# Low halves of the probabilities kept dense: products with values on 64 rows each, crossed over two banks

## The reference

```python
q = rope(layernorm(x) @ wq)      # 32 heads of 128
k = rope(ctx @ wk)               # 8 heads, each shared by 4 query heads
v = ctx @ wv                     # 8 heads
attn = softmax(q @ k.T / sqrt(128) + mask)
x = x + tanh(g_xattn) * ((attn @ v) @ wo)
h = layernorm(x)
# one of 8 experts for each position, chosen by the largest logit, of rank 16:
x = x + tanh(g_ffn) * (top_logit * (h @ A[e].T) @ Bw[e].T)
```

## Time and profile before

| | |
|---|---|
| median of 3 runs | 1091.52 us (1091.41 to 1092.5) |
| span of the profiled execution, first to last instruction | 1089.0 us |
| PE busy | 1082.4 us (99%) |
| PE weight loads busy | 919.3 us (84%) |
| DVE busy | 874.1 us (80%) |
| ACT busy | 636.8 us (58%) |
| POOL busy | 591.9 us (54%) |
| share of PE in the chain that ended last | 97% |
| granted TensorE clock | 9 tenths or more in all 40 slices; mean 1.000 |

### The profile page before, as it was taken

The page is one execution under the profiler, slowest core; times in us unless marked ns, Lnnn a source line. Parts: engine busy times, 40 slices in busy tenths (PEclk is TensorE's granted clock), DMA queues, the critical chain, the costliest instruction groups (busy, mean ns, idle before and its releaser), DMA issues.

```text
span 1089.0 us, 17107 instructions
## 1 busy us (share of the span) xinstructions
PE 1082.4 (99%) x5640; PEld 919.3 (84%) x5640; DVE 874.1 (80%) x1423; ACT 636.8 (58%) x1112; POOL 591.9 (54%) x518
## 2 busy tenths in 40 slices
PE   9999999999999999999999999999999999999998
PEld 7888888888888888888888888888888888888886
DVE  7876657888888888888887898777777777777887
ACT  7563476586666666666655545555555555555553
POOL 5552379888877777777754433333333333333423
PEclk9999999999999999999999999999999999999999
DMA  7858964496646464646489546553535353543112
GB/s 258 273 210 336 391 220 183 155 379 201 214 155 213 155 213 156 212 156 212 141 300 380 185 136 205 177 187 111 187 110 187 112 184 114 179 116 118 40 39 78
DMA packets 106087, 206.27 MB, mean 189 GB/s; under 512 B 8849, under 2 KB 58641, under 8 KB 100113
## 3 DMA queue, kind: packets, MB, share of 16 engines
q1 hardware_dynamic: 105424, 204.40, 55.2%
q10 hardware_dynamic: 576, 0.79, 0.2%
HBM read 122.31 MB, written 82.84 MB: 188 GB/s over the span
## 4 chain that ended last, share of the span: by engine, by line
PE 97%; DVE 2%; DMA 0%; issue 0%; ACT 0%; DVEq 0%; SPq 0%
PE attn L945 32%; PE proj L877 28%; PE score L894 10%; PE attn L839 8%; PE score L839 4%; PE turned L839 4%; PE attn L930 3%; PE attn L932 3%; PE turned L905 3%; PE proj L811 1%; PE small L983 1%; PE small L1008 1%; PE score L983 0%; DMA near_raw<-in_ctx 0%; DVE o_s L1270 0%; DVE stats L1140 0%
## 5 line engine op out<-in xcount | busy, mean ns | idle before, releaser
L945 PE MATMUL attn<-wo_s,o_s 128*128 128x512 f32 x1524 | 374.7, 395 | 0.2 <-DVE o_s L1270 0.2
L877 PE MATMUL proj<-xB,wq_s 128*128 128x512 f32 x1344 | 332.6, 391 | 0.0
L945 PEld LDWEIGHTS attn<-wo_s,o_s 128*128 128x128 f32 x1524 | 280.9, 188 | 57.0 <-DVE o_s L1270 0.4
L877 PEld LDWEIGHTS proj<-xB,wq_s 128*128 128x128 f32 x1344 | 252.0, 188 | 51.3 <-issue 0.2
L1863 POOL TENSOR_TENSOR rot<-rot,tab 128x512 f32<-128x512 f32 x110 | 162.3, 1475 | 145.2 <-ACT rot L1584 145.0
L1633 ACT ACTIVATE o_s<-attn 128x512 fp32r<-128x512 f32 x127 | 69.3, 595 | 112.2 <-PE attn L932 112.1
L894 PEld LDWEIGHTS score<-k_r,q_r 128*128 128x128 f32 x1024 | 123.9, 191 | 5.5 <-DVE q_r L1180 0.4
L1175 DVE TENSOR_TENSOR q_r<-q_r,tab 128x512 f32<-128x512 f32 x127 | 120.9, 952 | 1.5 <-ACT x_third L1584 1.4
L894 PE MATMUL score<-k_r,q_r 128*128 128x64 f32 x1024 | 121.3, 271 | 0.0
L1605 ACT ACTIVATE copies<-proj 128x512 f32<-128x512 f32 x96 | 57.5, 599 | 78.0 <-PE proj L877 77.8
L1282 DVE SCALAR_TENSOR_TENSOR acc<-attn,gates_t,acc 128x512 f32<-128x512 f32 x127 | 94.8, 747 | 4.1 <-PE attn L945 1.2
(11 more groups left out here) (269 smaller groups left out, 1681.5 us busy)
## 6 DMA issues: line engine op xcount, KB each, us to landing
wq_kept<-wq_s SPq DMA_DIRECT2D x16, 1792.0 KB, 6.3
wq_s<-wq_kept SPq DMA_DIRECT2D x16, 1792.0 KB, 8.2
v_kept<-vst SPq DMA_DIRECT2D x64, 256.0 KB, 4.3
v_s<-v_kept SPq DMA_DIRECT2D x128, 128.0 KB, 5.0
wo_kept<-wo_s SPq DMA_DIRECT2D x32, 512.0 KB, 5.7
wo_s<-wo_kept SPq DMA_DIRECT2D x32, 512.0 KB, 5.2
k_kept<-kst SPq DMA_DIRECT2D x32, 256.0 KB, 2.2
wq_raw<-in_wq SPq DMA_DIRECT2D x16, 512.0 KB, 7.8
```

Of the source, the lines that this page charges most:

```text
L877: last = e.matmul(dst[:, :], wq_s[:, b % 2, A, s, kt, :], xB[:, B, mv, kt, :], start=(first and kt == 0 and m == 0), stop=(kt == 1 and m = ...
L945: last = e.matmul(out_bank(k, bp)[:, :], o_s[:, s, bp, h, :], wo_s[n % WO_SLOTS][:, m, :], start=(h == 0 and i == 0), stop=(h == GROUP - 1 ...
```

## The change

`p_low` loses its padding: for each pair of sequences it is 256 columns, in which both twins' low halves stand under each other, as they do in `turned`. POOL's memset of the zeros goes. The pass of 512 columns over 128 rows becomes two passes of 256 columns over 64 rows each, twin 0 with rows 0 to 63 of `p_low` and `v_both`, twin 1 with rows 64 to 127. Both twins of a pair write into one bank, and two passes on different rows of the array are not let into one bank at a time. So the passes are crossed: in turn 0 pair 0 does twin 0 (bank `attn0`) and pair 1 twin 1 (bank `attn1`); then PE waits until both have ended (new semaphore `lows_begun`); in turn 1 pair 0 does twin 1 and pair 1 twin 0. `times_values` is split into `times_high` (the passes of 256 columns over 128 rows, unchanged) and `times_low`. `attn_high` now waits for the last passes of both pairs. In DVE's program the two instructions of `prob_low`, which stood apart in most steps, stand together.

```diff
-        p_low = sb_at(base + 131072, "p_low", [P, PAIRS, 2, GROUP * SEQ], F32R)
+        p_low = sb_at(base + 131072, "p_low", [P, PAIRS, GROUP * SEQ], F32R)
...
-            def times_values(k, pairs=range(PAIRS)):
+            def times_high(k, pairs=range(PAIRS)):
...
-                e.wait_ge(probs_low, 2 * k + 2)
...
                     for twin in range(2):
-                        e.matmul(b[:, cols[twin]], v_s[:, u % 2, twin, tiles[bp], :], p_high[:, twin, cols[bp]],
-                                 start=(twin == 0), stop=False, skip_group_check=True)
-                    e.matmul(b[:, :], v_both[:, u % 2, tiles[bp], :], p_low[:, bp].rearrange("p t n -> p (t n)"),
-                             start=False, stop=True, skip_group_check=True).then_inc(values_used, 1)
+                        e.matmul(out_bank(k, bp)[:, TWIN_COLS[twin]], v_s[:, u % 2, twin, sub * PAIRS + bp, :],
+                                 p_high[:, twin, TWIN_COLS[bp]], start=(twin == 0), stop=False, skip_group_check=True)
+
+            def times_low(k):
+                u, sub = divmod(k, SUBS)
+                e.wait_ge(probs_low, k + 1)
+
+                for turn in range(2):
+                    if turn:
+                        e.wait_ge(lows_begun, PAIRS * (k + 1))
+                    for bp in range(PAIRS):
+                        twin = bp if turn == 0 else 1 - bp
+                        rows = TWIN_ROWS[twin]
+                        e.matmul(out_bank(k, bp)[:, TWIN_COLS[twin]], v_both[rows, u % 2, sub * PAIRS + bp, :], p_low[rows, bp],
+                                 start=False, stop=(turn == 1), skip_group_check=True).then_inc((lows_begun, values_used)[turn], 1)
...
-            times_values(k + 1, [0])
+            times_high(k + 1, [0])
             scores(k + 3)
-            times_values(k + 1, [1])
+            times_high(k + 1, [1])
+            times_low(k + 1)
...
-            def prob_low(k, *twins):
...
+            def prob_low(k):
+                e.wait_ge(probs_high, 3 * k + 2)
...
+                for twin, rows in enumerate(TWIN_ROWS):
+                    last = e.tensor_tensor(p_low[rows, :, :], turned[rows, :].rearrange("p (b n) -> p b n", b=PAIRS),
+                                           p_high[rows, twin, :].bitcast(F32).rearrange("p (b n) -> p b n", b=PAIRS), ALU.subtract)
+                last.then_inc(probs_low, 1)
...
-                together = k % 4 == 3 or (k, 6) in EXTRA
-                if not together:
-                    prob_low(k, 0)
+                if not (k % 4 == 3 or (k, 6) in EXTRA):
+                    prob_low(k)
...
-                prob_low(k, *((0, 1) if together else (1,)))
+                if k % 4 == 3 or (k, 6) in EXTRA:
+                    prob_low(k)
...
             def attn_high(k, bp):
-                e.wait_ge(values_used, PAIRS * k + bp + 1)
+                e.wait_ge(values_used, PAIRS * (k + 1))
...
-                if n == ZEROS_BESIDE:
-
-                    e.wait_ge(rope_added, FOUR.stop)
-                    e.memset(p_low[:, :, :, :].bitcast(F32), 0.0).then_inc(zeros_set, 1)
```

More of the change, by code:

```diff
@@ L43 @@
 SPLIT_PRODUCTS = ((0, 0), (0, 1), (1, 0))
+TWIN_COLS = (slice(0, GROUP * SEQ), slice(GROUP * SEQ, 2 * GROUP * SEQ))
 TWIN_ROWS = (slice(0, SEQ), slice(SEQ, 2 * SEQ))
@@ L195 @@
 SCORES_AFTER = 62
-FOUR_UNTIL, ZEROS_BESIDE = 63, 63
+FOUR_UNTIL = 63
 ROPE_BESIDE = {51: (0, 0), 54: (0, 1), 55: (0, 2), 56: (0, 3), 57: (1, 0), 60: (1, 1), 61: (1, 2)}
@@ L430, in build @@
         mix_scaled, out_ready_g = sem("mix_scaled"), sem("out_ready_g")
-        zeros_set, warm_zeros = sem("zeros_set"), sem("warm_zeros")
+        warm_zeros, lows_begun = sem("warm_zeros"), sem("lows_begun")
         power_set, ln_rstd, times_sin, less_max = sem("power_set"), sem("ln_rstd"), sem("times_sin"), sem("less_max")
@@ L906, in turn_probs @@
                 last.then_inc(probs_turned, 1)
-                drained[turned.name] = probs_low, 2 * k + 2
-            def times_values(k, pairs=range(PAIRS)):
-                u, s = divmod(k, SUBS)
-                tiles = [s * PAIRS + bp for bp in range(PAIRS)]
+                drained[turned.name] = probs_low, k + 1
+            def times_high(k, pairs=range(PAIRS)):
+                u, sub = divmod(k, SUBS)
                 e.wait_ge(v_in[u % 2], 80 * (u // 2 + 1))
-                e.wait_ge(probs_low, 2 * k + 2)
                 e.wait_ge(probs_high, 3 * k + 3)
-                cols = [slice(bp * GROUP * SEQ, (bp + 1) * GROUP * SEQ) for bp in range(PAIRS)]
                 for bp in pairs:
@@ L927, in times_values @@
                         e.wait_ge(x1_added, 2 * k - 1 + bp)
-                    b = out_bank(k, bp)
                     for twin in range(2):
-                        e.matmul(b[:, cols[twin]], v_s[:, u % 2, twin, tiles[bp], :], p_high[:, twin, cols[bp]],
-                                 start=(twin == 0), stop=False, skip_group_check=True)
-                    e.matmul(b[:, :], v_both[:, u % 2, tiles[bp], :], p_low[:, bp].rearrange("p t n -> p (t n)"),
-                             start=False, stop=True, skip_group_check=True).then_inc(values_used, 1)
+                        e.matmul(out_bank(k, bp)[:, TWIN_COLS[twin]], v_s[:, u % 2, twin, sub * PAIRS + bp, :],
+                                 p_high[:, twin, TWIN_COLS[bp]], start=(twin == 0), stop=False, skip_group_check=True)
+            def times_low(k):
+                u, sub = divmod(k, SUBS)
+                e.wait_ge(probs_low, k + 1)
[7 more added lines that the diff above has]
+                                 start=False, stop=(turn == 1), skip_group_check=True).then_inc((lows_begun, values_used)[turn], 1)
+            def times_values(k):
+                times_high(k)
+                times_low(k)
             def project_out(k, bp):
@@ L974, in expert @@
                     elif t >= HALF_TILES + 2:
-                        e.wait_ge(probs_low, 2 * STEPS)
+                        e.wait_ge(probs_low, STEPS)
                         e.wait_ge(x1_added, 2 * (STEPS - 1))
@@ L1252, in sum_rows @@
                 e.reciprocal(row_inv[:, k % 2, :], row_sum[:, k % 2, :]).then_inc(inverted, 1)
-            def prob_low(k, *twins):
[L1255 to L1264, removed]
+            def prob_low(k):
+                e.wait_ge(probs_high, 3 * k + 2)
+                if k:
+                    e.wait_ge(values_used, PAIRS * k)
+                else:
+                    e.wait_ge(rope_added, FOUR.stop)
+                for twin, rows in enumerate(TWIN_ROWS):
+                    last = e.tensor_tensor(p_low[rows, :, :], turned[rows, :].rearrange("p (b n) -> p b n", b=PAIRS),
+                                           p_high[rows, twin, :].bitcast(F32).rearrange("p (b n) -> p b n", b=PAIRS), ALU.subtract)
+                last.then_inc(probs_low, 1)
             def attn_low(k, bp):
@@ L1398, in _ @@
                 q_sum(*q)
-            prob_low(0, 0, 1)
+            prob_low(0)
             finish_key(len(JOBS) - 1)
@@ L1463, in _ @@
             add_out(k - 1, 0)
-            prob_low(k, 0, 1)
+            prob_low(k)
             sum_rows(k + 1)
@@ L1470, in _ @@
             mask_scores(k + 2)
-            prob_low(k + 1, 0, 1)
+            prob_low(k + 1)
             add_out(k, 0)
@@ L1482, in _ @@
             expert_norms_end(tiles_of(k)[1:])
-            prob_low(k + 2, 0, 1)
+            prob_low(k + 2)
             sum_rows(k + 3)
@@ L1492, in _ @@
             expert_norms_begin(tiles_of(k + 1)[:1])
-            prob_low(k + 3, 0, 1)
+            prob_low(k + 3)
             expert_norms_begin(tiles_of(k + 1)[1:])
```

## The result

| | before | changed | ratio, 95% interval |
|---|---|---|---|
| median of runs, us | 1091.47 (1090.84 to 1092.5) | 1127.91 (1125.49 to 1128.5) | 1.0327 [1.0313, 1.0342] |
| span of the profiled execution, us | 1089.0 | 1126.7 | |
| PE busy, us | 1082.4 | 1112.9 | |
| DVE busy, us | 874.1 | 874.9 | |
| ACT busy, us | 636.8 | 636.7 | |

A forecast was written before the change was run, and what follows sets the result against it. PE was taken to bound the kernel: 0.99 less 0.46 is 0.53 us a step, 33.9 us in 64 steps, plus 1.8 in the last steps, on 1089.0: 1124.7 us span; with 2.5 for the median, 1127 us, range 1100 to 1147.

The forecast's parts named there:

- PE bounds the kernel, so each step's loss counts 64 times: Whole loop: PE is busy throughout the steps, so 0.53 us more a step moves the end by 33.9 us.
- The change of row grouping, 0.166 us each, load beside the tail: Before and after the low passes: each switch between 128 and 64 rows costs one tail, 0.166 us; the load is hidden.
- Rival 1: Low passes: grouping change free, loads one behind the other; 0.304 us more a step, 1113 us; chance 0.28.
- Rival 2: Low passes: full restart at each grouping change, loads one behind the other; 0.84 us more a step, 1147 us; chance 0.17.
- The second pair's passes 0.106 us apart: After the wait between turns: the fourth low pass starts 0.106 us behind the third, because loads follow each other.
- Semaphore 0.05 us: Between the turns: from the end of the first two low passes to the third's load, 0.05 us.
- Uncovered load 0.104 us behind the wait: Third low pass: its weight load isn't pulled ahead of the wait and adds 0.104 us.
- The last steps, 1.8 us: Steps 60 and 61: without query products as cover, PE waits for DVE's o_s, 0.81 and 1.03 us more.
- DVE's, ACT's, POOL's part at zero: Other engines: prob_low's new order, the later rotary sum and the memset's removal cost nothing, since these engines have room.
- Rival 3: Low passes: perfect pairs and free grouping changes; 0.09 us more a step, 1099.5 us; chance 0.07.
- Rival 4: Low passes: PE's wait on its own passes is short; 0.18 us less a step, about 1081 us; chance 0.05.
- Wrong if the four starts lie within 0.46 us: Sign in the profile after: four low-pass starts in a step within 0.46 us would refute the forecast.

The follow-up runs named there:

- own_wait: As order_alone (padded passes), but PE waits before the second low pass until its first has ended; 1117.46 us, ratio 1.0241 to the kernel before.
- one_turn: The changed kernel without turn 0: two passes of 64 rows a step, no wait of PE on itself, half the low products left out; 1096.84 us, ratio 1.0053.
- same_rows: The changed kernel with all four low passes on rows 0 to 63, one behind the other, without the wait on itself; 1120.64 us, ratio 1.0267.
- the dummies: Two runs: the kernel before with 161 added passes of 256 columns, over 128 rows (1112.31 us) or over 64 rows (1173.52 us).
- filled: The changed kernel with the first query product placed between the two turns in steps 0 to 58, covering the wait; 1142.29 us, ratio 1.0475.
- dummy64: The kernel before with 161 added passes of 256 columns over rows 0 to 63, among the query products' passes; 1173.52 us, ratio 1.0757.
- order_alone: The kernel before with padded low passes of 128 rows, but all highs before both lows, and attn_high waiting for both pairs; 1094.29 us, ratio 1.0030.
- after_again: The changed kernel run once more, unaltered, on the chip of one_inc and filled; 1128.23 us, ratio 1.0342.
- one_inc: The changed kernel with one semaphore increment a turn less: only turn 0's second pass counts lows_begun up, and PE waits for it; 1125.81 us, ratio 1.0322.

## Why the prediction was right

Forecast 1127, measured 1127.91 us; a step was to cost 0.53 us more and costs 0.51. How near the last figure came is in part luck: the span was forecast at 1124.7 us and measured at 1126.7. The clock (1.6 us) and the first stage (1.3 us) were in no term, the steps cost 1.0 us less, and the median lies 1.2 us over the profiled span where 2.5 were taken. By its steps:

- *PE bounds the kernel, so each step's loss counts 64 times.* Right: own_wait, one_turn, same_rows and the dummies all came out within 3 us of a count of passes times a duration from a row; filled did not, as a second cost was missing there.
- *The change of row grouping, 0.166 us each, load beside the tail.* That the change stops the stream was right; the size was too small, and what it is made of was wrong. dummy64 gives 0.38 us for forth and back, 0.19 each: the load of the new grouping doesn't go beside the tail but starts near its end, and its 0.10 us are not covered; of the tail's 0.166 us only some 0.09 count. That 0.19 lies near the 0.166 forecast is luck. Rival 1 (no price, in its favour) fell with dummy64 and one_turn. Rival 2 had the right mechanism here, but a whole tail and a whole load; the load starts 0.07 us ahead of the modelled end of the tail. The Trainium skill, "TensorEngine Tiling (Array Packing)", section Tiling Modes, names a drain at a change of tiling mode; dummy64 agrees, with 0.19 us for each.
- *The second pair's passes 0.106 us apart.* Wrong: they start together. The scores' rows, from which I took the spacing, are loads for the same rows of the array; loads for different halves run beside each other, and two pairs take 0.38 us each. The Trainium skill, "TensorE: Matmul & The Clock Gate", Part 3, has passes on different row groups start about 4 ns apart; the trace agrees, as two passes take the 0.38 us of one.
- *Semaphore 0.05 us.* Too small: it was 0.09, and 0.06 in own_wait; with one increment in place of two it fell by 0.025.
- *Uncovered load 0.104 us behind the wait.* Right: 381 against 282 ns for the pass.

So three terms of the chain were off, by 0.11 us too much and by 0.09 too little in sum, and nearly cancelled: luck again. The ledger of a step, from the runs: columns saved 4 x 0.116 less 2 x 0.116 = -0.23; two changes of grouping +0.38; the wait on itself +0.36 (tail 0.166, semaphore 0.09, load 0.10). Together +0.51. By this ledger either of the two costs alone is more than the saving: 0.15 us lost a step without the wait, 0.13 without the changes. Neither of these two kernels was run; the figures are sums of the ledger.

- *The last steps, 1.8 us.* Right where it was placed: 0.8 in step 60 (0.81 forecast), 1.1 in step 61 (1.03 forecast), and order_alone has the waits without any pass of 64 rows. Missed was what such a wait can set off, the clock.
- *DVE's, ACT's, POOL's part at zero.* Right: DVE's and ACT's busy times are unchanged, POOL's is 2.3 us less, and order_alone shows no wait in the loop. DVE's own new order wasn't tried by itself, but in the changed kernel none of PE's waits is for p_low.
- Rival 3 had its pairs right and the change wrong. Rival 4 fell with own_wait and by its own sign: the third pass starts 0.47 us behind the first (414.27 to 414.74), not under 0.34.
- *The signs.* "Wrong if the four starts lie within 0.46 us" was a poor one: they lie within 0.47 us, since the passes of a pair start together. It had been set for passes 0.106 us apart. The stretch from the first high pass to the product, 1.44 against 1.02 us, tells the outcomes apart.

## What to carry to other kernels

A pass over half the rows pays only if the array stays in that grouping long enough: on this chip going there and back costs 0.38 us, over three passes of 256 columns. As an estimate from these numbers: each pair of half passes that replaces a padded pass of 512 columns saves 0.116 us, so at least four such pairs must follow each other without a wait. Zeros in a stream that PE runs without a gap are cheap, since a padded pass of 512 columns is 0.23 us, half of it for the zeros, while a PE that waits for its own result pays tail, semaphore and load, here 0.36 us. Before filling such a wait with other work, look at who stands behind the moved passes: in filled, the reader of the result became late in every step.

## What the runs showed of the hardware

- Passes over different halves of the array run fully beside each other, loads too: 0.38 us for two, as for one.
- A change of row grouping costs 0.38 us there and back, 0.19 on average, in a stream without other waits (61.2 us for 161 pairs of changes).
- A short gap can be followed by a lower clock. In the changed kernel PE, after the wait of step 60, ran at a granted clock of 0.5 (1.2 in place of 2.4 GHz) for 3.4 us and lost 1.6 us; in order_alone, with a wait of 0.97 us at the same place, it stayed at 1.00. after_again and same_rows had the same half clock at the same place, after waits of 0.86 and 0.83 us; one_inc and one_turn had none after 0.86 and 0.85 us. So the length of that wait doesn't decide it, and what does stays open.
